# New orders ahead of the experts for TensorE, ScalarE and VectorE, units split in halves, and input transfers ahead of the start counts

## The reference

```python
xn = layernorm(x)                                     # over the 512 features
q = xn @ w_q; k, v = split(xn @ w_kv)                 # 16 heads, 4 groups, head size 128
attn = softmax(causal(q @ k.T * 128**-0.5)) @ v @ w_dense
s = sigmoid(xn @ Wr.T + br)                           # 32 experts in 8 groups of 4
# a group's weight: its two largest s; the best 4 groups stay; the best 6 experts of those
gate = 2.5 * s[chosen] / sum(s[chosen])
moe = sum_e gate[:, e] * (relu(xn @ W1[e].T)**2 @ W2[e].T)   # hidden size 256
shared = relu(xn @ Ws1.T)**2 @ Ws2.T                         # hidden size 512
out = x + attn + shared + moe
```

## Time and profile before

| | |
|---|---|
| median of 3 runs | 1538.15 us (1534.75 to 1538.18) |
| the profiled execution's own time | 1538.73 us |
| its span in the profile | 1537.0 us |
| TensorE, matmuls | 1514.3 us busy, 99% |
| VectorE | 1134.0 us, 74% |
| ScalarE | 839.0 us, 55% |
| GpSimd | 296.0 us, 19% |
| mean granted TensorE clock | 0.995 |

### The profile page before, as it was taken

The page is one execution under the profiler, slowest core; times in us unless marked ns, Lnnn a source line. Parts: engine busy times, 40 slices in busy tenths (PEclk is TensorE's granted clock), DMA queues, the critical chain, the costliest instruction groups (busy, mean ns, idle before and its releaser), DMA issues.

```text
span 1537.0 us, 31138 instructions
## 1 busy us (share of the span) xinstructions
PE 1514.3 (99%) x8548; PEld 1304.8 (85%) x8549; DVE 1134.0 (74%) x2586; ACT 839.0 (55%) x1753; POOL 296.0 (19%) x540
## 2 busy tenths in 40 slices
PE   8998999999999999999999999999999999999998
PEld 7886888889989878888888888888888888888886
DVE  6796566666665669949948967976985994994896
ACT  4655666666666735635635644554553563563553
POOL 0001444434444301012002102102101101200211
PEclk8999999999999999999999999999999999999999
DMA  7692677777776621102102112512210210210111
GB/s 276 261 396 89 198 245 234 230 245 224 243 247 218 225 76 55 56 15 81 34 27 75 34 34 81 192 61 76 68 41 28 71 52 20 75 34 27 55 42 55
DMA packets 64774, 184.34 MB, mean 120 GB/s; under 512 B 7136, under 2 KB 7264, under 8 KB 60000
## 3 DMA queue, kind: packets, MB, share of 16 engines
q1 hardware_dynamic: 39888, 112.56, 21.0%
q0 software_dynamic: 16640, 54.54, 13.1%
q10 hardware_dynamic: 8208, 16.78, 2.8%
HBM read 123.29 MB, written 60.56 MB: 120 GB/s over the span
## 4 chain that ended last, share of the span: by engine, by line
PE 96%; DVE 3%; issue 0%; ACT 0%; DMA 0%; DVEq 0%; ACTq 0%; POOLq 0%
PE bank L665 9%; PE bank L667 9%; PE bank L666 9%; PE bank L989 8%; PE ps_s L665 7%; PE ps_s L667 7%; PE ps_s L666 6%; PE ps_s L976 5%; PE ps_s L978 4%; PE ps_s L977 4%; PE ps_s L857 4%; PE ps_s L880 3%; PE ps_s L861 3%; PE ps_s L858 3%; PE ps_s L884 3%; PE ps_s L881 3%
## 5 line engine op out<-in xcount | busy, mean ns | idle before, releaser
L1294 ACT ACTIVATE probs<-probs,negmax 128x128 f32<-128x128 f32 (+7 forms) x256 | 197.5, 774 | 122.6 <-DVE negmax L1702 122.0
L1302 ACT ACTIVATE pT_hi<-bank 128x512 fp32r<-128x512 f32 x288 | 164.3, 594 | 143.6 <-PE bank L989 117.6
L1321 DVE TENSOR_TENSOR pT_lo<-bank,pT_hi 128x512 fp32r<-128x512 f32 x288 | 189.7, 684 | 41.0 <-ACT pT_hi L1302 40.1
L1702 DVE CUSTOM_DVE_ANT_0 probs<-ps_s,causal 128x128 f32<-128x128 f32 (+7 forms) x256 | 189.4, 753 | 17.2 <-PE ps_s L978 15.0
L427 POOL TENSOR_TENSOR settled<-ident 128x1 f32<-128x1 f32 x192 | 45.0, 234 | 789.0 <-DVE acc L1731 779.1
L989 PE MATMUL bank<-ident,probs 128*128 128x128 f32 x1152 | 157.0, 272 | 0.0
L989 PEld LDWEIGHTS bank<-ident,probs 128*128 128x128 f32 x1152 | 136.9, 141 | 19.9
L665 PE MATMUL ps_s<-xT_hi,wa_hi 128*128 128x512 f32 x384 | 152.7, 398 | 0.0
L667 PE MATMUL ps_s<-xT_hi,wa_lo 128*128 128x512 f32 x384 | 151.0, 393 | 0.0
L666 PE MATMUL ps_s<-xT_lo,wa_hi 128*128 128x512 f32 x384 | 150.2, 391 | 0.0
L1711 DVE TENSOR_SCALAR probs<-probs,rnorm 128x128 f32<-128x128 f32 (+7 forms) x256 | 133.4, 521 | 9.1
(11 more groups left out here) (197 smaller groups left out, 3601.3 us busy)
## 6 DMA issues: line engine op xcount, KB each, us to landing
eraw<-we SPq DMA_DIRECT2D x37, 1024.0 KB
expert_outputs<-ysb SPq DMA_DIRECT2D x111, 256.0 KB
araw<-wa SPq DMA_DIRECT2D x37, 512.0 KB, 4.3
expert_outputs<-comb ACTq DMA_DIRECT2D x1, 16384.0 KB, 48.9
normed_tokens<-xn SPq DMA_DIRECT2D x4, 1024.0 KB, 9.2
out<-acc SPq DMA_DIRECT2D x16, 256.0 KB
acc<-x SPq DMA_DIRECT2D x2, 1024.0 KB, 13.8
turned_tokens<-xT_hi SPq DMA_DIRECT2D x2, 1024.0 KB, 5.5
```

What stands on the lines that cost most here:

```text
L1294: act.activation(pr, pr, ACT.Exp, bias=negmax[:, i % 2, a:a + 1], scale=-1.0, accum_out=rowsum[:, i % 2, a:a + 1]).then_inc(exp_ready, 1)
L1302: act.activation(pT_hi[:, blk % RING, :], ps_t[blk % 2][:, :], ACT.Copy).then_inc(pt_hi_ready, 1)
L1321: dve.tensor_tensor(out_, whole, upper.bitcast(F32), ALU.subtract).then_inc(signal, 1)
L1702: dve.tensor_tensor_reduce(halves(probs[:, i % 2, a, 0:keys]), ps_s[:, s:s + parts, 0:keys // parts], halves(causal[:, SQ - keys:]), -1.0, ...
```

## The change

On GpSimd the constants now come ahead of the start counts. SyncE issues all input loads (x, the router's weights, the shared network's weights) without a wait for `started`, and waits for it ahead of its first store. TensorE, ScalarE and VectorE wait for `started` only at the end of this stage. TensorE waits for two of the constants (identity and triangle) in place of all six, and for the router's weights at the first logits. `square_unit` is split into `square_unit(j, m)` and `upper_unit(j, m)`, `lower_unit` becomes `lower_unit(j, m)`, and `outputs(o, 0)` waits for each half of its two units just ahead of that half's matmuls. All three engines have new orders. The first `warm` has 12 matmuls in place of 16, and the later ones 2, 2, 6 and 2 in place of four times 2. The arithmetic is the same. Shown in full is TensorE's order; of ScalarE's and VectorE's the pieces of which the prediction speaks.

```diff
-WARM = 16
+WARM = 12
...
         def _(sp):
-            sp.wait_ge(started, 4)
             residual = (res1, acc)
             def load_part(i):
...
+            sp.wait_ge(started, 4)
             for s in range(B):
                 for h in range(2):
                     sp.wait_ge(xn_ready, s * NT + (h + 1) * HALF)
...
         def _(pool):
+            pool.memset(ones[:, :].bitcast(F32), 1.0).then_inc(ones_ready, 1)
+            pool.memset(y_gate[:, 0, :], 1.0).then_inc(pool_chain, 1)
...
+            pool.memset(scan_ones[:, :], 1.0).then_inc(consts_ready, 1)
+            pool.tensor_copy(lane[:, :], tok_idx[:, 0:MAXT]).then_inc(consts_ready, 1)
+            pool.tensor_copy(tok_f[:, :], tok_i[:, :]).then_inc(consts_ready, 1)
+
             for s in start_at_one:
                 pool.sem_inc(s, 1)
...
         def _(pe):
-            pe.wait_ge(started, 4)
-
             def split_product(out_, lhs, rhs, parts, n_inc, first=True, last=True):
...
             warm(WARM)
-            pe.wait_ge(consts_ready, 6)
-            pe.wait_ge(consts_in, 32)
+            pe.wait_ge(consts_ready, 2)
...
+                if s == 0 and t == 0:
+                    pe.wait_ge(consts_in, 32)
                 if s and t == 0:
...
                 if q == 0:
-                    pe.wait_ge(hlo_ready, (o + 1) * NSH * KM)
                     pe.wait_ge(ew_lo, NSH * WP)
...
                 qs = slice(q * P, (q + 1) * P)
-                part = lambda k: ((o * NSH + k // KM) % HR, k // KM, k % KM)
-                split_product(ps_out[n % 2][:, :],
-                              lambda k: (h_hi[:, part(k)[0], part(k)[2], qs], h_lo[:, part(k)[0], part(k)[2], qs]),
-                              lambda k: (w2(hi_slot(part(k)[1]))[:, part(k)[2], :], w2(lo_slot(part(k)[1]))[:, part(k)[2], :]),
-                              NSH * KM, y_ready)
+                for k in range(NSH * KM):
+                    u, m = divmod(k, KM)
+                    if q == 0:
+                        pe.wait_ge(hlo_ready, o * NSH * KM + k + 1)
+                    h_h, h_l = (h[:, (o * NSH + u) % HR, m, qs] for h in (h_hi, h_lo))
+                    w_h, w_l = (w2(slot(u))[:, m, :] for slot in (hi_slot, lo_slot))
+                    pe.matmul(ps_out[n % 2][:, :], h_h, w_h, start=(k == 0), stop=False)
+                    pe.matmul(ps_out[n % 2][:, :], h_h, w_l, start=False, stop=False)
+                    mm = pe.matmul(ps_out[n % 2][:, :], h_l, w_h, start=False, stop=(k == NSH * KM - 1))
+                mm.then_inc(y_ready, 1)
             def ranks():
                 pe.wait_ge(sel_ready, B)
+                pe.wait_ge(consts_ready, 6)
...
             turn_up(0, 1)
+            warm(2)
             logits(0, 0)
             warm(2)
             turn_up(0, 2)
+            turn_up(0, 3)
+            warm(6)
             logits(0, 1)
             warm(2)
-            turn_up(0, 3)
             logits(0, 2)
-            warm(2)
+            turn_up(0, 4)
             logits(0, 3)
-            warm(2)
-            hidden(0, 0)
-            hidden(0, 1)
-            turn_up(0, 4)
             turn_up(0, 5)
             logits(0, 4)
             turn_up(0, 6)
             logits(0, 5)
             turn_up(0, 7)
             logits(0, 6)
+            hidden(0, 0)
+            hidden(0, 1)
             hidden(1, 0)
             logits(0, 7)
+            turn_up(1, 0)
             hidden(1, 1)
-            turn_up(1, 0)
             turn_up(1, 1)
+            turn_up(1, 2)
+            hidden(2, 0)
+            hidden(2, 1)
+            hidden(3, 0)
+            hidden(3, 1)
             logits(1, 0)
-            hidden(2, 0)
-            turn_up(1, 2)
+            turn_up(1, 3)
+            turn_up(1, 4)
             logits(1, 1)
-            turn_up(1, 3)
+            turn_up(1, 5)
             logits(1, 2)
-            hidden(2, 1)
-            turn_up(1, 4)
+            turn_up(1, 6)
+            turn_up(1, 7)
             logits(1, 3)
-            hidden(3, 0)
-            turn_up(1, 5)
             logits(1, 4)
-            turn_up(1, 6)
             logits(1, 5)
-            hidden(3, 1)
-            turn_up(1, 7)
             logits(1, 6)
             logits(1, 7)
             outputs(0, 0)
             outputs(0, 1)
+            hidden(4, 0)
             outputs(0, 2)
             outputs(0, 3)
-            hidden(4, 0)
+            ranks()
             hidden(4, 1)
-            ranks()
             outputs(1, 0)
             outputs(1, 1)
+            hidden(5, 0)
+            hidden(5, 1)
+            list_rows(0)
+            list_rows(1)
             outputs(1, 2)
-            outputs(1, 3)
-            list_rows(0)
-            hidden(5, 0)
-            list_rows(1)
-            hidden(5, 1)
             list_rows(2)
             hidden(6, 0)
             list_rows(3)
+            list_rows(4)
             hidden(6, 1)
-            list_rows(4)
+            list_rows(5)
+            outputs(1, 3)
+            list_rows(6)
+            hidden(7, 0)
+            list_rows(7)
...
+            pe.wait_ge(started, 4)
...
         def _(act):
-            act.wait_ge(started, 4)
-
...
@@ scalar @@
             root(0)
             copy_up(0, 0)
-            upper_up(0, 0)
             copy_up(0, 1)
-            upper_up(0, 1)
             root(1)
             upper_shared(0, 0)
+            upper_up(0, 0)
+            copy_up(0, 2)
+            copy_up(0, 3)
+            upper_up(0, 1)
+            upper_up(0, 2)
+            root(2)
...
+            upper_unit(3, 0)
+            square_unit(3, 1)
+            upper_unit(3, 1)
             relu_unit(4, 0)
...
             relu_unit(7, 1)
-            square_unit(7)
             mark_rows(15)
-
+            square_unit(7, 1)
+            upper_unit(7, 0)
+            upper_unit(7, 1)
...
@@ vector @@
             spread(1)
             normalize(1)
+            spread(2)
             lower_up(0, 0)
+            normalize(2)
             lower_up(0, 1)
+            lower_up(0, 2)
...
+            route_experts(1)
             add_output(0, 2)
+            route_gates(1)
+            lower_up(1, 7)
+            lower_unit(2, 1)
+            lower_unit(3, 0)
             add_output(0, 3)
-            route_experts(1)
-            lower_unit(2)
-            lower_unit(3)
-            route_gates(1)
-            lower_up(1, 4)
-            lower_up(1, 5)
             count_tiles()
+            lower_unit(3, 1)
+            place_rows()
             add_output(1, 0)
...
+            mark_rows(13)
+            lower_unit(6, 1)
+            mark_rows(14)
             add_output(2, 2)
-            mark_rows(12)
-            mark_rows(13)
-            add_output(2, 3)
-            mark_rows(14)
             mark_rows(15)
-            lower_unit(7)
             dve.wait_ge(hot_used, TILES)
             dve.tensor_copy(tok_idx[:, 0:MAXT], ps_list).then_inc(list_ready, 1)
...
+            dve.wait_ge(started, 4)
+            lower_unit(7, 0)
+            lower_unit(7, 1)
+            add_output(2, 3)
+            add_output(3, 0)
             lower_weights(0, 0, slot_of(0))
+            add_output(3, 1)
+            add_output(3, 2)
             lower_weights(0, 1, slot_of(0))
-            add_output(3, 0)
             lower_weights(0, 2, slot_of(0))
             lower_weights(0, 3, slot_of(0))
-            add_output(3, 1)
-            add_output(3, 2)
             lower_tokens(0)
```

More of the change, by code:

```diff
@@ L607, in _ @@
             pool.tensor_copy(tok_f[:, :], tok_i[:, :]).then_inc(consts_ready, 1)
+            for s in start_at_one:
+                pool.sem_inc(s, 1)
+            for half in range(2):
+                pool.sem_inc(y_stored[half], 1)
+            pool.sem_inc(y_free, YB - 2)
+            pool.sem_inc(mx_ready, XG)
+            pool.sem_inc(xT_ok, 64)
+            pool.sem_inc(z_ok, 16 * NT)
+            pool.sem_inc(aw_hi, 3)
+            pool.sem_inc(aw_lo, 3)
+            pool.sem_inc(araw_in[0], 32)
+            pool.sem_inc(araw_in[1], 16)
+            pool.sem_inc(started, 4)
             pool.wait_ge(list_ready, 1)
@@ L1140, in _ @@
-            upper_shared(0, 2)
+            square_unit(0, 0)
+            relu_unit(0, 1)
+            upper_unit(0, 0)
+            root(4)
+            square_unit(0, 1)
             upper_shared(0, 3)
             relu_unit(1, 0)
-            root(4)
+            upper_unit(0, 1)
+            square_unit(1, 0)
+            copy_up(1, 0)
+            exponent(0)
             relu_unit(1, 1)
-            copy_up(1, 0)
+            upper_shared(1, 2)
+            upper_up(1, 0)
+            square_unit(1, 1)
@@ L1173, in _ @@
                           comb[:, COMB - 1, :].unsqueeze(1).to_broadcast([P, MAXT - MINT, D])).then_inc(y_filled, 16)
-            square_unit(3)
+            upper_unit(2, 0)
+            upper_unit(2, 1)
+            relu_unit(3, 1)
+            upper_up(1, 6)
+            square_unit(3, 0)
+            upper_up(1, 7)
+            upper_unit(3, 0)
```

(67 more changed lines are left out.)

131 lines of the change are left out of this document (48 added, 83 removed).

## The result

| | before | changed |
|---|---|---|
| median of 11 runs | 1538.15 us (1533.63 to 1540.21) | 1530.22 us (1524.62 to 1532.38) |
| ratio | | 0.995, 95% interval 0.9938 to 0.9963 |
| profiled execution, its span | 1538.73, 1537.0 us | 1530.99, 1529.2 us |
| half clock ahead of the first expert's tile | 10.2 and 3.4 us | 10.2 and 6.8 us |

The change is faster by 0.5%, 7.9 us at the median; forecast were 7.2 us and 1531 us.

A forecast was written before the change was run, and what follows sets the result against it. TensorE, busy 99% of the span, was taken as the bound, so time returns only from its idle or half-clock stretches. 5.6 - 3.4 + 0 + 5.0 + 1.0 - 1.0 = 7.2 us gave 1531 us, range 1526 to 1541 us.

The forecast's parts named there:

- Part 1: The start: input loads issued without the wait for `started`, so the first transposes start at 7.2 us; gain 2.2 us.
- Parts 2 and 3: First block: tiles 4 to 7 earlier, worth 5.6 us with the start at full clock; the clock's fall takes back 3.4.
- Part 4: From 33 us to `ranks`: the new order gains 0 at full clock; ends -1 and +2 us.
- case (c): Rival: both blocks of logits and transposes run at 1.2 GHz, so the kernel is slower, 1543 us; chance 0.14.
- (d): Rival: VectorE is late for `ranks` by 3 us, 1534 us; chance 0.10.
- Part 5: The list, `ranks` to `outputs(3, 0)`: gain 5.0 us from waits for tables, and 1.0 us from the clock behind the pause.
- the first term: The list: `outputs(3, 0)` comes sooner behind `ranks`, gain 5.0 us; ends 5.7 and 3.
- VectorE's walk: The list: VectorE's tables, additions and lower halves summed to 35.5 us, ending 50.7 us behind `ranks`.
- Part 6: The first expert: the third expert's weights are loaded later and ScalarE may wait; loss 1.0 us, ends 0 and 3.

The follow-up runs named there:

- kernel 3: The changed kernel, but `outputs(o, 0)` waits for all four halves of its two units ahead of its first product; 1533.22 us, ratio 0.9963.
- kernel 11: The kernel before with only the early start and the list's end (`add_output(2, 3)` behind the list's copy, `mark_rows(15)` ahead of `square_unit(7)`); 1527.49 us, ratio 0.9939.
- 8: The changed kernel with `hidden(3, .)` spread into the second block of transposes and logits, and 13 more warm products in the first block; 1533.08 us, ratio 0.9967.
- kernel 9: The changed kernel with 13 more warm products in the first block, no hidden passes moved; 1526.36 us, ratio 0.9920.
- kernel 2: The kernel before with only the list's end changed: `add_output(2, 3)` behind the list's copy, `mark_rows(15)` ahead of `square_unit(7)`; 1533.15 us, ratio 0.9967.
- 1: The kernel before with only the new start: constants ahead of the start counts, input loads and engines without a wait for them; 1536.15 us, ratio 0.9987.
- kernels 5 to 8: The changed kernel with `hidden(3, .)` spread into the second block (1537.99 us), `hidden(0, 0)` early (1527.66), both (1535.79), or the spread plus 13 warm products (1533.08).

## Why the prediction was right, point by point

- **Part 1, right.** 2.2 us forecast, 2.4 in the profile, 2.0 measured alone (0.3 to 3.5).
- **Parts 2 and 3, the sizes right, the reading half, the reason for the fall wrong.** Forecast was `hidden(1, 0)` at 27.9 us at full clock and 3.4 us lost to the clock. It came at 27.99 us in kernel 3, which kept the clock there, and at 31.17 in the changed kernel: 3.2 us lost. Against 33.56 before that is 2.4 us, but it is the start's shift and nothing more. I credited the new order with 5.6 us at full clock, of which about 5 were the old order's half clock. The old order without half clock, with the early start (kernel 11), reaches the same pass at 27.19 us, so at full clock the new one brings nothing there. The half clock had to be taken as a property of the execution, for both orders. I expected the fall because of a pause of 1.9 us ahead of the first transposes. The pause was 0.47 us, as the 12 warm products took 5.49 us in place of 4.3, and the kernels 3, 8 and 9 had pauses of 1.1 to 1.6 us and kept the clock in this block. That the fall came, and lasted 10 us, was luck. From the first transposes to `ranks` the old order without any half clock takes 66.4 - 2.75 = 63.6 us (kernel 2), and the new one 64.6 us with 6.8 us of it at half clock (kernel 3). The pass in the changed kernel, in 3 and in 11:

```profile
31.17 0.39 PE L663 MATMUL ps_s<-xT_hi,w_hi 128*128 128x512 f32 x1
...
27.99 0.39 PE L663 MATMUL ps_s<-xT_hi,w_hi 128*128 128x512 f32 x1
...
27.19 0.48 PE L664 MATMUL ps_s<-xT_hi,w_hi 128*128 128x512 f32 x1
```

- **Part 4, wrong by 1.1 us.** Forecast 0. The clock fell at 58.0 us within the five logits, which I had put into case (c) with 0.14, and was at half for 6.8 us. It cost some 0.6 us in the logits and 2.1 us in eleven products of `outputs(0, .)` at almost twice the distance. This fall goes with the order: nine of the ten profiles with the new orders have one between 48 and 61 us, and none of the four with the old (before, 1, 2, 11) has. The 1.2 us of idle time between 34 and 77 us (41.82 us busy of 43 in the kernel before and in 11, 43.00 in the changed one) came back against it. VectorE was ready for `ranks` 2.0 us ahead, so (d) did not happen.
- **Part 5, right in mechanism, too small.** 5.0 and 1.0 us forecast, 7.9 measured to the first expert's tile: 6.7 of it up to `outputs(3, 0)` (now at 129.75 us) and 1.2 behind, so the first term was too small. VectorE's walk was 1.8 us too slow: its last table ended at 129.30 us, 48.9 us behind the end of `ranks`, where 50.7 was forecast. That put the gain above its upper end, 5.7 us, too. The idle time understates what a wait costs: a product's busy time reads 0.39 us where the next starts 0.23 us behind it, and kernel 3's waits of 2.8 us in sum made its stretch 3.1 us longer. The list's end alone gives 4.8 of the 7.9 us. The halves are worth 3.1 in the new order, and I had costed them at nothing but the absence of a wait.

```profile
127.84 1.46 DVE L1527 TENSOR_SCALAR tile_hot<-lane,xf,tok_f 128x160 f16<-128x160 f16 x6
```

- **Part 6, the size by accident.** 1.0 us of loss forecast, 1.4 in the profile. The weights were issued at 141.01 us, about 11 us behind `outputs(3, 0)` as forecast, and ScalarE waited 1.8 us, but TensorE's loss was the clock's: kernels with late weights and no fall lose nothing. The kernel before had its 3.4 us of half clock ahead of the first expert's tile, the changed kernel behind it.
- **The clock in thin stretches.** It stayed full for 8 us of nothing but transposes and logits (49.8 to 58.0 us) and fell within five logits in a row. In the first block it came back only 1.8 to 4.4 us into the hidden passes, in every profile with a fall there. The Trainium skill, "TensorE: Matmul & The Clock Gate", Part 4, has transposes not count as activity in the same way as matmuls. For coming back the trace agrees; for holding the full clock, transposes between the logits did no visible harm here.

The errors were +1.1 us (part 4), -1.9 us (part 5) and under 0.5 elsewhere; they cancelled to 0.7 us. That the total came this close is luck in part.

## What to carry to other kernels

Where an engine is 99% busy, the next few microseconds lie in its clock as much as in its waits: profile several executions of both kernels before an order is credited with a stretch at full or half clock, and try more products of 512 columns in stretches of small ones, judged by the median of several executions (here 3.9 us lower). A step in an in-order queue can cover a wait on another engine that no view shows; look at what stands behind the late step before moving the cover. Of a large new order, test the two or three cheap pieces alone: here they matched the whole at the median.

## What the runs showed of the hardware

The time of one and the same kernel varies with its granted clock by about half of what the change is worth. Of 29 executions of the kernel before that ran beside kernels 5 to 8, the eleven with a mean granted clock of 0.997 or more took 1533.8 to 1537.1 us, the others 1538.0 to 1542.3. Of the list-end kernel, four executions at 0.999 or 1.00 took 1529.0 to 1529.5 us and the other eight 1532.8 to 1535.2. Thirteen products whose result nobody reads set the first hidden pass back by 1.9 us at full clock (22.95 us in kernel 9, 21.02 in kernel 3), and the kernel with them is 3.9 us lower at the median.
